# Layer 3's attention scores: the split queries stacked on 128 rows against the high keys, the low keys as a pair of 64-row products

## Chip, cores, metric

One NeuronCore of one Trainium2 chip. The metric is device time in microseconds (us) of one execution of the whole program; smaller is better.

## What is computed

Four layers in sequence on tokens `x` (2 x 1024 x 256) with a condition vector. Only layer 3's attention matters here; its part of the reference, cut:

```python
# on B = 2 sequences of N = 1024 tokens, D = 256;  H, HD = 16, 64
h = _ln(x, ln1_g, ln1_b) + shift
qkv = (h @ Wqkv.T).reshape(b, n, 3, H, HD)
q = _ln(qkv[:, :, 0].transpose(0, 2, 1, 3), qn_g, qn_b)
k = _ln(qkv[:, :, 1].transpose(0, 2, 1, 3), kn_g, kn_b)
v = qkv[:, :, 2].transpose(0, 2, 1, 3)
scores = jnp.einsum('bhnd,bhmd->bhnm', q, k) / jnp.sqrt(jnp.float32(HD))
attn = jax.nn.softmax(scores, axis=-1)
o = jnp.einsum('bhnm,bhmd->bhnd', attn, v)
x = x + o.transpose(0, 2, 1, 3).reshape(b, n, H * HD) @ Wout.T
...   # then a mixture of experts
```

## The kernel before

The program runs its stages one after another. Each stage has a block with one instruction stream per engine; the order within each is written out in the code, and semaphores tie the streams together. The two stages that the change touches are `layer3_qkv` (projections, normalisation of each head, writing of Q, K and V to device memory) and the heads stage of layer 3 (`heads_stage` with the class `Heads`), which follows it.

To keep the accuracy of 32 bits with the faster type float32r, an operand is split into a high part (rounded) and a low part (the rest), and a product is the sum of three: high x high, high x low, low x high. `PASSES = ((0, 0), (0, 1), (1, 0))` lists them. Device memory holds `l3_q` and `l3_k` as (part, head, 64, 1024): 64 features on rows, 1024 tokens along the row, each part 256 KB for a head.

`Heads` works through 32 heads (2 sequences x 16) of 8 turns each, 256 turns g in all; a turn has 128 queries t against 1024 keys. In SBUF a head has `Q` (128 partitions x 2 parts x 1024) and `K` (128 x 2 x 512). Partitions 0 to 63 and 64 to 127 both hold all the queries, in both parts; the keys are divided: the upper half has keys 0 to 511, the lower half keys 512 to 1023. So a product on rows 0 to 63 gives the scores of the first 512 keys, and one on rows 64 to 127 those of the others, and the two run in the array at once, as a pair. There are two such sets of tiles: `k3first` and `q3first` for even heads, `l3h_K` and `l3h_Q` for odd ones.

What each engine does in the heads stage:

- TensorE, for each g: `score(g)` (line 1477, six products of 512 columns; it waits for the exponentials of turn g - 2, and at a head's first turn for the head's loads), `turn(g - 3)` (line 1488, sixteen 64-row transposes of the probabilities into `ring`, waiting for the scaling and for both engines' copies of the turn before), and `mix` (line 1500, two products of the values with the transposed probabilities of the head before, each written as two instructions, with 128 rows and 64 columns of weights each). The mix starts at turn 11.
- VectorE: the negated maximum of each score row (line 1534), the inverse of the sum (line 1540), and the copy of one half of the transposes (line 1524).
- ScalarE: its half of the transposes (line 1526), the exponential with its sum (line 1558), and once a head `ocopy`, which copies the head's result to `osb` (line 1548). `osb` has two buffers; the copy of head n waits until the result of head n - 2 is stored.
- GpSimd: the scaling of the probabilities (line 1568), and in some turns a piece of the output weights' split.
- SP issues the transfers, in this order for each n: `load(n + 1)`, which is four times `load_head_part` (lines 1393 and 1394, one piece of Q and one of K), after the last score of head n - 1; `store(n - 2)` (line 1446, two transfers from `osb`); `load_v(n + 1)` (line 1440), after the mix of head n - 1; from n = 20 on for some heads one load of results for the next stage into `o3T` (line 1974).

In `layer3_qkv`, TensorE makes the sums of q, k and v for each tile of 128 tokens with products of 128 rows and 512 columns (line 2289), and transposes the normalised heads in 64-row halves (line 2256). Its inputs are a normalised chunk of 512 tokens in high and low parts, in two buffers (`NormTurnParts`). SP loads head 0's Q and K there, in four steps at the tiles 9 to 12 (`load_head_part` again).

Of the kernel before, what the change touches and what calls it, by code (L numbers as in the profile page):

```python
# [21 lines left out]
P = 128  # L22
# [1365 lines left out]
def load_head_part(sp, tiles, parts, n, part, hd, loaded):  # L1388

    (K, Q), (q, k) = tiles, parts  # L1390
    p_, c = divmod(part, 2)
    r = slice(c * hd, (c + 1) * hd)
    sp.dma_start(Q[r, p_, :].bitcast(F32), q[p_, n, :, :]).then_inc(loaded, 16)
    sp.dma_start(K[r, p_, :].bitcast(F32), k[p_, n, :, c * C:(c + 1) * C]).then_inc(loaded, 16)


class Heads:
# [3 lines left out]
    LOADS = 8  # L1401

    def __init__(self, s, parts, V, out, ident, hd, vscale, tiles, pending):
        self.V, self.out, self.ident, self.hd, self.vscale = V, out, ident, hd, vscale
        self.pending = pending
        self.K, self.Q = ([t, s.sb(n, shape, F32R)] for t, n, shape in zip(tiles, "KQ", ([P, 2, C], [P, 2, S])))
        self.vs = s.sb("vs", [P, 2, TB, hd])
        self.prob = s.sb("prob", [P, 4, S])
        self.pT = s.sb("pT", [P, 2, TB, S])
        self.osb = s.sb("osb", [P, 2, C])  # L1410
        self.nmax, self.total, self.inv = (s.sb(n, [P, 4]) for n in ("nmax", "total", "inv"))
        self.score = [s.ps(f"score{i}", (P, S)) for i in range(2)]
# [17 lines left out]
    def sp_program(self, sp):  # L1430
        def load(n):
            u = n % 2
            self.need(sp, self.scores, TB * (n - 1))
            for part in range(4):
                load_head_part(sp, (self.K[u], self.Q[u]), (self.q, self.k), n, part, self.hd, self.loaded[u])
# [7 lines left out]
        def store(n):  # L1443
            sp.wait_ge(self.ocopied, n + 1)
            for c in range(2):
                sp.dma_start(self.out[n, :, c * C:(c + 1) * C],
                             self.osb[c * self.hd:(c + 1) * self.hd, n % 2, :]).then_inc(self.stored[n % 2], 16)
# [19 lines left out]
    def pe_program(self, pe):  # L1467
        def score(g):
            n, t = divmod(g, TB)
            u = n % 2  # L1470
            if t == 0:
                self.need(pe, self.loaded[u], (n // 2 + u) * 16 * self.LOADS)
            self.need(pe, self.exps, g - 1)
            for i, (x, y) in enumerate(PASSES):
                for c in range(2):
                    r = slice(c * self.hd, (c + 1) * self.hd)
                    mm = pe.matmul(self.score[t % 2][:, c * C:(c + 1) * C], self.Q[u][r, x, t * P:(t + 1) * P],  # L1477
                                   self.K[u][r, y, :], start=i == 0, stop=i == 2)
            mm.then_inc(self.scores, 1)
# [64 lines left out]
    def act_program(self, act):  # L1544
        def ocopy(n):
            act.wait_ge(self.outs, n + 1)
            self.need(act, self.stored[n % 2], 32 * (n // 2))
            act.activation(self.osb[:, n % 2, :], self.ob[n % 2][:, :], ACT.Copy).then_inc(self.ocopied, 1)
# [620 lines left out]
class NormTurnParts(NormTurn):  # L2169

    def __init__(self, *args, **kw):
        super().__init__(*args, **kw)
        s, name = args[0], kw.get("name", "norm")
        self.parts = [s.sb(f"{name}_{n}", [P, self.bufs, KF, C], F32R) for n in ("hi", "lo")]
        self.written, self.split = s.sem(f"{name}_written"), s.sem(f"{name}_split")

    def act_scale(self, act, c):
# [3 lines left out]
        for kf in range(KF):  # L2181
            act.wait_ge(self.turned, c * KF + kf + 1)
            for to, sem in ((self.out[:, c % self.bufs, kf, :], self.written), (self.parts[0][:, c % self.bufs, kf, :], self.ready)):
# [3 lines left out]
    def dve_split(self, dve, c):  # L2187
        for kf in range(KF):
            dve.wait_ge(self.written, c * KF + kf + 1)
            dve.wait_ge(self.ready, c * KF + kf + 1)  # L2190
            dve.tensor_tensor(self.parts[1][:, c % self.bufs, kf, :], self.out[:, c % self.bufs, kf, :],
                              self.parts[0][:, c % self.bufs, kf, :].bitcast(F32), ALU.subtract).then_inc(self.split, 1)
# [5 lines left out]
def layer3_qkv(nc, sems, g, w, o):  # L2198
# [4 lines left out]
    with Stage(nc, sems, "l3qkv") as s:  # L2203
# [3 lines left out]
        nt = NormTurnParts(s, X, g["gain3"], g["shift3"], ident, [tb[:, kf * C:(kf + 1) * C] for kf in range(KF)], 1e-5)  # L2207
# [19 lines left out]
        def _(sp):  # L2227
            o.sp_results(sp, 1)
            o.sp_inverses(sp, 1)
            for tt in range(T):  # L2230
# [11 lines left out]
                if TB < tt <= TB + 4:  # L2242
                    load_head_part(sp, (g["k3first"], g["q3first"]), g["q3k3"], 0, tt - TB - 1, HD, early)
            sp.wait_ge(early, 8 * 16)

        @block.tensor
        def _(pe):
# [26 lines left out]
            for tt in range(T):  # L2274
# [3 lines left out]
                for j in range(6):  # L2278
# [8 lines left out]
                    for kf in range(KF):  # L2287
                        for p_, (x, y) in enumerate(PASSES):
                            mm = pe.matmul(sumb[i][:, half * C:(half + 1) * C], nt.parts[x][:, c % 2, kf, t * P:(t + 1) * P],
# [690 lines left out]
def build(nc, d, out):  # L2980
# [9 lines left out]
    with ExitStack() as always:  # L2990
# [22 lines left out]
        with ExitStack() as layer2:  # L3013
# [25 lines left out]
            with ExitStack() as weights3:  # L3039
                sb(weights3, "w3oT", [P, H * 64 // P * D])  # L3040
                sb(weights3, "k3first", [P, 2, C], F32R)
                sb(weights3, "q3first", [P, 2, S], F32R)
                with Semaphores(nc) as sems:
# [15 lines left out]
                    for name, shape, dt in (("o3T", [P, 2, H * 64 // P, C], F32), ("w3o_hi", [P, H * 64 // P * D], F32R),  # L3059
# [4 lines left out]
                                (g["k3first"], g["q3first"]), g["l3_pending"])  # L3064
# [24 lines left out]
```

## Time and profile before

| | |
|---|---|
| runs of the kernel | 2115.70, 2118.59, 2133.62 us (median 2118.59) |
| the profiled execution | 2115.73 us, span 2114.0 us |
| granted TensorE clock, mean over the span | 0.921 |
| busy share of the span | TensorE 89%, VectorE 70%, ScalarE 56%, GpSimd 38% |
| heads stage of layer 3 | first score at 1219.8, last at about 1830 us |

The profile is one execution, recorded by the hardware, with times from the span's start. PE is TensorE's products, PEld its weight loads, DVE is VectorE, ACT ScalarE, POOL GpSimd, SPq SP's transfers. A row names the line of the kernel, the output and inputs by the program's names, and the shape: `64*128 64x512` is a load of 64 rows by 128 columns of weights with 64 x 512 of the moving operand. "Idle before" tells how long the engine had nothing to do before a group, and what ended that. The end of a product is modelled: it holds the way through the array, so that products that follow closely overlap in the rows.

### The profile page before, as it was taken

To read this page: it belongs to the slowest core of one execution; us is meant where nothing else is said; L and a number is where in the kernel's file an instruction comes from. 1 tells how busy PE (TensorE), PEld (TensorE's weight loads), DVE (VectorE), ACT (ScalarE), POOL (GpSimd) and SP (SyncE) were. 2 spreads that over 40 slices of the span, in tenths; PEclk is the share of its full clock that TensorE was granted. 3 is DMA by queue.
4 is the path that set the end of the run, shared out by engine and by line. 5 is a ranking of instruction groups with operands and counts; after the bars stand their busy time and mean duration, and the time that the engine had idled before them with its cause. 6 is when DMAs were issued, how large, how long until landed. Compare 5 with 4: busy or idle time off the path is not lost. (4 is left out here: it accounts for less than half of the span.)

```text
span 2114.0 us, 37287 instructions
## 1 busy us (share of the span) xinstructions
PE 1873.8 (89%) x14338; PEld 1192.7 (56%) x14338; DVE 1483.4 (70%) x2500; ACT 1188.8 (56%) x2038; POOL 805.5 (38%) x724
## 2 busy tenths in 40 slices
PE   6988999788989999996888889999999999993786
PEld 3766577677533333333666655555555555492686
DVE  5665743564479897984688777777777777546796
ACT  3332332332228686884556677777777777632463
POOL 3465620174040302001245645554444444304376
PEclk8999999899959897998899989999999999996798
DMA  5000000100533211212256954454445555225453
GB/s 148 0 4 17 3 18 0 61 1 1 154 96 93 49 39 37 55 32 67 90 185 213 298 140 101 112 121 113 101 108 131 127 125 141 61 80 160 140 150 51
DMA packets 196833, 191.40 MB, mean 91 GB/s; under 512 B 64240, under 2 KB 155248, under 8 KB 196400
## 3 DMA queue, kind: packets, MB, share of 16 engines
q1 hardware_dynamic: 193584, 184.82, 32.4%
q0 software_dynamic: 3072, 4.20, 1.1%
q8 instruction: 114, 1.87, 0.4%
q14 instruction: 63, 0.52, 0.1%
HBM read 121.33 MB, written 67.37 MB: 89 GB/s over the span
## 5 line engine op out<-in xcount | busy, mean ns | idle before, releaser
L1568 POOL TENSOR_SCALAR l3h_prob<-l3h_prob,l3h_inv 128x1024 f32<-128x1024 f32 x256 | 288.2, 1126 | 320.8 <-DVE l3h_inv L1540 320.8
L1534 DVE TENSOR_REDUCE l3h_nmax<-l3h_score 128x1 f32<-128x1024 f32 x256 | 313.5, 1225 | 138.0 <-PE l3h_score L1477 137.9
L1758 DVE TENSOR_REDUCE l2h_nm<-l2h_rowb 128x1 f32<-128x1024 f32 x256 | 302.7, 1218 | 43.0 <-PE l2h_rowb L1689 42.7
L1793 ACT ACTIVATE l2h_pT<-l2h_score 128x512 f32<-128x512 f32 x512 | 274.7, 597 | 97.0 <-PE l2h_score L1711 74.5
L1558 ACT ACTIVATE l3h_prob<-l3h_score,l3h_nmax 128x1024 f32<-128x1024 f32 x256 | 285.8, 1117 | 38.5 <-DVE l3h_nmax L1534 3.6
L1500 PE MATMUL l3h_out<-l3h_pT,l3h_vs 128*64 128x512 f32 x1024 | 274.4, 617 | 0.0
L1526 ACT ACTIVATE l3h_pT<-l3h_ring 128x512 f32<-128x512 f32 x256 | 152.8, 597 | 104.4 <-PE l3h_ring L1488 103.9
L1488 PEld LDWEIGHTS l3h_ring<-ident,l3h_prob 64*128 64x128 f32 x4096 | 173.2, 139 | 35.5 <-issue 8.0
L1524 DVE COPY l3h_pT<-l3h_ring 128x512 f32<-128x512 f32 x256 | 172.1, 672 | 2.0 <-PE l3h_ring L1488 2.0
L1488 PE MATMUL l3h_ring<-ident,l3h_prob 64*128 64x64 f32 x4096 | 169.4, 222 | 2.2 <-DVE l3h_pT L1524 2.0
L1725 PE MATMUL l2h_out<-l2h_pT,l2h_vs 128*32 128x256 f32 (+1 forms) x1792 | 166.1, 445 | 0.0
L2492 POOL TENSOR_TENSOR l3qkv_lo<-l3qkv_full,l3qkv_hi 128x1024 fp32r<-128x1024 f32 x32 | 99.3, 3102 | 108.7 <-ACT l3qkv_hi L2327 108.7
L1477 PE MATMUL l3h_score<-k3first,q3first 64*128 64x512 f32 x768 | 125.0, 432 | 9.6 <-PEq L68 6.3
L1477 PEld LDWEIGHTS l3h_score<-k3first,q3first 64*128 64x128 f32 x768 | 63.7, 188 | 114.6 <-issue 99.8
L1477 PE MATMUL l3h_score<-l3h_K,l3h_Q 64*128 64x512 f32 x768 | 123.0, 425 | 2.5 <-DMA l3h_K<-l_k 2.3
L1477 PEld LDWEIGHTS l3h_score<-l3h_K,l3h_Q 64*128 64x128 f32 x768 | 62.1, 184 | 109.1 <-issue 96.0
L1689 PE MATMUL l2h_rowb<-l2K,l2Q 48*128 48x512 f32 x256 | 103.0, 499 | 13.8 <-PEq L68 9.6
L1711 PE MATMUL l2h_score<-l2Q,l2K 50*128 50x512 f32 x256 | 105.6, 497 | 0.5
L1807 POOL COPY l2h_vs<-V 128x128 f32<-128x128 f32 x32 | 8.3, 294 | 237.5 <-PE l2h_out L1725 237.5
L1689 PEld LDWEIGHTS l2h_rowb<-l2K,l2Q 48*128 48x128 f32 x256 | 44.6, 214 | 76.4 <-DVE l2h_nm L1758 60.6
L1725 PEld LDWEIGHTS l2h_out<-l2h_pT,l2h_vs 128*32 128x32 f32 x1792 | 36.4, 110 | 82.8 <-issue 51.2
L2380 DVE TENSOR_SCALAR l3qkv_full<-l3qkv_turns,headln 128x1024 f32<-128x1024 f32 x32 | 42.9, 1340 | 37.2 <-PE l3qkv_turns L2256 37.2
(456 smaller groups left out, 4354.4 us busy)
## 6 DMA issues: line engine op xcount, KB each, us to landing
q3first<-l_q SPq DMA_DIRECT2D x64, 256.0 KB, 5.1
l3h_Q<-l_q SPq DMA_DIRECT2D x64, 256.0 KB, 5.0
l_q<-l3qkv_hi SPq DMA_DIRECT2D x16, 512.0 KB, 4.7
l_q<-l3qkv_lo SPq DMA_DIRECT2D x16, 512.0 KB, 3.4
l_k<-l3qkv_hi SPq DMA_DIRECT2D x16, 512.0 KB, 3.0
l_k<-l3qkv_lo SPq DMA_DIRECT2D x16, 512.0 KB, 3.0
k3first<-l_k SPq DMA_DIRECT2D x64, 128.0 KB, 5.1
l3h_vs<-l_v SPq DMA_DIRECT2D x32, 256.0 KB, 3.1
```

Source lines behind the costliest of these rows:

```text
L1477: mm = pe.matmul(self.score[t % 2][:, c * C:(c + 1) * C], self.Q[u][r, x, t * P:(t + 1) * P], self.K[u][r, y, :], start=i == 0, stop=i == 2)
L1488: mm = pe.transpose(self.ring[half][:, kk * P // 2:(kk + 1) * P // 2], self.prob[r, g % 4, kk * P:(kk + 1) * P], self.ident[r, r])
L1500: mm = pe.matmul(self.ob[n % 2][c * self.hd:(c + 1) * self.hd, :], self.vs[:, n % 2, kk, :], self.pT[:, n % 2, kk, c * C:(c + 1) * C], sta ...
L1524: eng.tensor_copy(dst, src).then_inc(self.emptied_d, 1)
L1526: eng.activation(dst, src, ACT.Copy).then_inc(self.emptied_a, 1)
L1534: dve.tensor_reduce(self.nmax[:, t % 4:t % 4 + 1], self.score[t % 2][:, :], AX.X, ALU.max, negate=True).then_inc(self.maxes, 1)
L1558: act.activation(self.prob[:, q, :], self.score[g % 2][:, :], ACT.Exp, bias=self.nmax[:, q:q + 1], accum_out=self.total[:, q:q + 1]).then_ ...
L1568: pool.tensor_scalar(self.prob[:, q, :], self.prob[:, q, :], self.inv[:, q:q + 1], self.vscale, ALU.mult, ALU.mult).then_inc(self.scaled, 1)
L1689: mm = pe.matmul(self.rowb[h][:, c * C:(c + 1) * C], self.Q[u][r:r + self.SPLIT, t * P:(t + 1) * P], self.K[u][r:r + self.SPLIT, c * C:(c ...
L1725: mm = pe.matmul(self.ob[r:r + self.mw, at:at + w], self.vs[:, m % self.SLOTS, h, k, :], self.pT[:, g % 4, h, c * C + at:c * C + at + w], ...
L1758: dve.tensor_reduce(self.nm[:, mr % 2, at:at + 1], self.rowb[h][:, :], AX.X, ALU.max, negate=True).then_inc(self.maxes, 1)
L1793: act.activation(self.pT[:, g % 4, h, c * C:(c + 1) * C], self.score[v % 3][:, :], ACT.Exp).then_inc(self.exps, 1)
```

## The change

The queries and keys of a head are laid out differently, and the three parts of the score are made in another grouping.

- `Q[:, 0, :]` now has the high queries on partitions 0 to 63 and the low queries on 64 to 127. `K` has the high keys, all 1024, on both halves. One product over 128 rows gives high x high plus low x high at once, for 512 keys; two such products give the whole score row (`c` = 0, 1).
- The third part, high queries x low keys, stays a pair of 64-row products: `KL` has the low keys 0 to 511 on the upper half and 512 to 1023 on the lower, and the lower half needs the high queries too, which are loaded into `Q[64:128, 1]`.
- So a score has four products instead of six: full, full, and a pair. A head's loads are three of Q (256 KB each), two of K (256 KB) and two of `KL` (128 KB) where they were four of Q (256 KB) and four of K (128 KB).
- `K` and `KL` together need more room in SBUF. It is found by giving `osb` one buffer instead of two (the copy of head n now waits for the store of head n - 1), and by letting head 0's `KL` tile (`k3lo`) serve in `layer3_qkv` as one of the four pieces of the normalised chunk's low part.

The diff, without the changes of names in the calls:

```diff
 def load_head_part(sp, tiles, parts, n, part, hd, loaded):
-    (K, Q), (q, k) = tiles, parts
-    p_, c = divmod(part, 2)
-    r = slice(c * hd, (c + 1) * hd)
-    sp.dma_start(Q[r, p_, :].bitcast(F32), q[p_, n, :, :]).then_inc(loaded, 16)
-    sp.dma_start(K[r, p_, :].bitcast(F32), k[p_, n, :, c * C:(c + 1) * C]).then_inc(loaded, 16)
+    (K, KL, Q), (q, k) = tiles, parts
+    up, down = slice(0, hd), slice(hd, 2 * hd)
+    if part < 2:
+        r = (up, down)[part]
+        sp.dma_start(Q[r, 0, :].bitcast(F32), q[part, n, :, :]).then_inc(loaded, 16)
+        sp.dma_start(K[r, :, :].rearrange("p a c -> p (a c)").bitcast(F32), k[0, n, :, :]).then_inc(loaded, 16)
+    elif part == 2:
+        sp.dma_start(Q[down, 1, :].bitcast(F32), q[0, n, :, :]).then_inc(loaded, 16)
+    else:
+        for c, r in enumerate((up, down)):
+            sp.dma_start(KL[r, :].bitcast(F32), k[1, n, :, c * C:(c + 1) * C]).then_inc(loaded, 16)
...
 class Heads:
-    LOADS = 8
+    LOADS = 7
...
-        self.K, self.Q = ([t, s.sb(n, shape, F32R)] for t, n, shape in zip(tiles, "KQ", ([P, 2, C], [P, 2, S])))
+        self.Q = [tiles[2], s.sb("Q", [P, 2, S], F32R)]
...
-        self.osb = s.sb("osb", [P, 2, C])
+        self.K, self.KL = [tiles[0], s.sb("K", [P, 2, C], F32R)], [tiles[1], s.sb("KL", [P, C], F32R)]
+        self.osb = s.sb("osb", [P, C])
...
                 sp.dma_start(self.out[n, :, c * C:(c + 1) * C],
-                             self.osb[c * self.hd:(c + 1) * self.hd, n % 2, :]).then_inc(self.stored[n % 2], 16)
+                             self.osb[c * self.hd:(c + 1) * self.hd, :]).then_inc(self.stored[n % 2], 16)
...
-            for i, (x, y) in enumerate(PASSES):
-                for c in range(2):
-                    r = slice(c * self.hd, (c + 1) * self.hd)
-                    mm = pe.matmul(self.score[t % 2][:, c * C:(c + 1) * C], self.Q[u][r, x, t * P:(t + 1) * P],
-                                   self.K[u][r, y, :], start=i == 0, stop=i == 2)
+            for c in range(2):
+                pe.matmul(self.score[t % 2][:, c * C:(c + 1) * C], self.Q[u][:, 0, t * P:(t + 1) * P],
+                          self.K[u][:, c, :], start=True, stop=False)
+            for c in range(2):
+                r = slice(c * self.hd, (c + 1) * self.hd)
+                mm = pe.matmul(self.score[t % 2][:, c * C:(c + 1) * C], self.Q[u][r, c, t * P:(t + 1) * P],
+                               self.KL[u][r, :], start=False, stop=True)
             mm.then_inc(self.scores, 1)
...
             act.wait_ge(self.outs, n + 1)
-            self.need(act, self.stored[n % 2], 32 * (n // 2))
-            act.activation(self.osb[:, n % 2, :], self.ob[n % 2][:, :], ACT.Copy).then_inc(self.ocopied, 1)
+            self.need(act, self.stored[(n + 1) % 2], 32 * ((n + 1) // 2))
+            act.activation(self.osb[:, :], self.ob[n % 2][:, :], ACT.Copy).then_inc(self.ocopied, 1)
...
 class NormTurnParts(NormTurn):
-        self.parts = [s.sb(f"{name}_{n}", [P, self.bufs, KF, C], F32R) for n in ("hi", "lo")]
+        self.hi, lo = s.sb(f"{name}_hi", [P, self.bufs, KF, C], F32R), s.sb(f"{name}_lo", [P, self.bufs * KF - 1, C], F32R)
+        self.lo = [[first_low[:, :] if n == 0 else lo[:, n - 1, :] for n in range(u * KF, (u + 1) * KF)] for u in range(self.bufs)]
...
+    def part(self, x, c, kf):
+        return self.lo[c % self.bufs][kf] if x else self.hi[:, c % self.bufs, kf, :]
...
 def layer3_qkv(nc, sems, g, w, o):
                 if TB < tt <= TB + 4:
-                    load_head_part(sp, (g["k3first"], g["q3first"]), g["q3k3"], 0, tt - TB - 1, HD, early)
-            sp.wait_ge(early, 8 * 16)
+                    load_head_part(sp, (g["k3first"], g["k3lo"], g["q3first"]), g["q3k3"], 0, tt - TB - 1, HD, early)
+            sp.wait_ge(early, 7 * 16)
```

## Rows read from the trace of the kernel before

**Rows 1.** The page: its header and part 1.

```profile
span 2114.0 us, 37287 instructions
...
PE 1873.8 (89%) x14338; PEld 1192.7 (56%) x14338; DVE 1483.4 (70%) x2500; ACT 1188.8 (56%) x2038; POOL 805.5 (38%) x724
```

**Rows 2.** Busy time of each engine in two stretches, granted clock, DMA.

```profile
1400.00:1600.00 200.00, 200.00 (x2180) 113.86 (x2180) 157.18 (x250) 155.02 (x262) 94.10 (x84) 1.00 0.49 112
640.00:700.00 60.00, 59.33 (x524) 21.78 (x520) 57.30 (x57) 52.30 (x99) 1.60 (x6) 1.00 0.38 95
```

**Rows 3.** Timeline of one turn: start us, duration us, engine, line, operation [idle before].

```profile
1502.39 0.96 PE L1477 MATMUL l3h_score<-l3h_K,l3h_Q 64*128 64x512 f32 x6
1502.96 0.74 PEld L1488 LDWEIGHTS l3h_ring<-ident,l3h_prob 64*128 64x128 f32 x16
...
1503.39 1.23 DVE L1534 TENSOR_REDUCE l3h_nmax<-l3h_score 128x1 f32<-128x1024 f32 x1 [0.51 <-PE l3h_score L1477]
...
1504.61 0.67 DVE L1524 COPY l3h_pT<-l3h_ring 128x512 f32<-128x512 f32 x1
...
1504.78 0.53 PEld L1477 LDWEIGHTS l3h_score<-l3h_K,l3h_Q 64*128 64x128 f32 x6 [0.81 <-issue]
...
1505.36 0.74 PEld L1488 LDWEIGHTS l3h_ring<-ident,l3h_prob 64*128 64x128 f32 x16
```

**Rows 4.** Timeline in four short windows of that turn.

```profile
1502.39 0.50 PE L1477 MATMUL l3h_score<-l3h_K,l3h_Q 64*128 64x512 f32 x2
...
1502.73 0.62 PE L1477 MATMUL l3h_score<-l3h_K,l3h_Q 64*128 64x512 f32 x4
...
1503.78 0.65 PE L1500 MATMUL l3h_out<-l3h_pT,l3h_vs 128*64 128x512 f32 x2
...
1504.26 0.60 PE L1500 MATMUL l3h_out<-l3h_pT,l3h_vs 128*64 128x512 f32 x2
```

**Rows 5.** Line L1477 from 1243 to 1850: durations ns min/median/max; who waited (us, times).

```profile
L1477 PE MATMUL l3h_score<-l3h_K,l3h_Q x744: 386/390/501, 1243.9 to 1830.8; 64*128 64x512 f32 x186
...
  DVE l3h_nmax L1534: 129.5, 244
```

**Rows 6.** Timeline in layer 3's projections, TensorE's products, then its weight loads.

```profile
1200.57 0.39 PE L2289 MATMUL l3qkv_k_sum<-w3lo,l3qkv_norm_hi 128*128 128x512 f32 x1
1200.80 0.40 PE L2289 MATMUL l3qkv_k_sum<-w3hi,l3qkv_norm_lo 128*128 128x512 f32 x1
...
1201.77 0.50 PE L2289 MATMUL l3qkv_v_sum<-w3hi,l3qkv_norm_hi 128*128 128x512 f32 x1
1202.11 0.39 PE L2289 MATMUL l3qkv_v_sum<-w3lo,l3qkv_norm_hi 128*128 128x512 f32 x1
...
1201.13 0.58 PEld L2256 LDWEIGHTS l3qkv_turns<-ident,l3qkv_xn 64*128 64x128 f32 x16 [0.36 <-issue]
1201.77 0.19 PEld L2289 LDWEIGHTS l3qkv_v_sum<-w3hi,l3qkv_norm_hi 128*128 128x128 f32 x1
```

**Rows 7.** Timeline of TensorE in the stage's first turns.

```profile
1238.62 0.71 PE L1488 MATMUL l3h_ring<-ident,l3h_prob 64*128 64x64 f32 x16 [0.33 <-DVE l3h_pT L1524]
```

**Rows 8.** Waits from 1260 to 1840: us in all, times, longest us.

```profile
PEld l3h_score L1477 <- DMA l3h_K<-l_k: 7.5, 6, 2.0
PEld l3h_score L1477 <- DMA k3first<-l_k: 5.9, 5, 1.7
```

**Rows 9.** Timeline around the start of a late head.

```profile
1644.19 0.36 SPq L1440 DMA_DIRECT2D l3h_vs<-l_v  x1
...
1649.63 0.60 SPq L1394 DMA_DIRECT2D l3h_K<-l_k  x1
...
1650.27 1.23 SPq L1446 DMA_DIRECT2D l_heads_out<-l3h_osb  x2
...
1657.26 0.96 PE L1477 MATMUL l3h_score<-l3h_K,l3h_Q 64*128 64x512 f32 x6 [1.12 <-DMA l3h_K<-l_k]
...
1665.41 0.59 ACT L1548 ACTIVATE l3h_osb<-l3h_out 128x512 f32<-128x512 f32 x1
```

More of the change, by code:

```diff
@@ L1434, in load @@
             for part in range(4):
-                load_head_part(sp, (self.K[u], self.Q[u]), (self.q, self.k), n, part, self.hd, self.loaded[u])
+                load_head_part(sp, (self.K[u], self.KL[u], self.Q[u]), (self.q, self.k), n, part, self.hd, self.loaded[u])
         def load_v(n):
@@ L2169, with __init__ @@
 class NormTurnParts(NormTurn):
-    def __init__(self, *args, **kw):
+    def __init__(self, first_low, *args, **kw):
         super().__init__(*args, **kw)
         s, name = args[0], kw.get("name", "norm")
-        self.parts = [s.sb(f"{name}_{n}", [P, self.bufs, KF, C], F32R) for n in ("hi", "lo")]
+        self.hi, lo = s.sb(f"{name}_hi", [P, self.bufs, KF, C], F32R), s.sb(f"{name}_lo", [P, self.bufs * KF - 1, C], F32R)
+        self.lo = [[first_low[:, :] if n == 0 else lo[:, n - 1, :] for n in range(u * KF, (u + 1) * KF)] for u in range(self.bufs)]
         self.written, self.split = s.sem(f"{name}_written"), s.sem(f"{name}_split")
@@ L2182, in act_scale @@
             act.wait_ge(self.turned, c * KF + kf + 1)
-            for to, sem in ((self.out[:, c % self.bufs, kf, :], self.written), (self.parts[0][:, c % self.bufs, kf, :], self.ready)):
+            for to, sem in ((self.out[:, c % self.bufs, kf, :], self.written), (self.hi[:, c % self.bufs, kf, :], self.ready)):
                 act.activation(to, self.banks[kf][:, :], ACT.Identity, bias=self.shift[:, kf, b:b + 1],
@@ L2190, in dve_split @@
             dve.wait_ge(self.ready, c * KF + kf + 1)
-            dve.tensor_tensor(self.parts[1][:, c % self.bufs, kf, :], self.out[:, c % self.bufs, kf, :],
-                              self.parts[0][:, c % self.bufs, kf, :].bitcast(F32), ALU.subtract).then_inc(self.split, 1)
+            dve.tensor_tensor(self.lo[c % self.bufs][kf], self.out[:, c % self.bufs, kf, :],
+                              self.hi[:, c % self.bufs, kf, :].bitcast(F32), ALU.subtract).then_inc(self.split, 1)
+    def part(self, x, c, kf):
+        return self.lo[c % self.bufs][kf] if x else self.hi[:, c % self.bufs, kf, :]
     def wait_split(self, eng, c):
@@ L2206, in layer3_qkv @@
         sumb = [s.ps(f"{n}_sum", (P, W)) for n in ("q", "k", "v")]
-        nt = NormTurnParts(s, X, g["gain3"], g["shift3"], ident, [tb[:, kf * C:(kf + 1) * C] for kf in range(KF)], 1e-5)
+        nt = NormTurnParts(g["k3lo"], s, X, g["gain3"], g["shift3"], ident, [tb[:, kf * C:(kf + 1) * C] for kf in range(KF)], 1e-5)
         qk = s.sb("qk", [P, 2, 2 * W])
@@ L2288, in _ @@
                         for p_, (x, y) in enumerate(PASSES):
-                            mm = pe.matmul(sumb[i][:, half * C:(half + 1) * C], nt.parts[x][:, c % 2, kf, t * P:(t + 1) * P],
+                            mm = pe.matmul(sumb[i][:, half * C:(half + 1) * C], nt.part(x, c, kf)[:, t * P:(t + 1) * P],
                                            wp[y][:, (kf * 6 + j) * C:(kf * 6 + j + 1) * C],
@@ L3042, in build @@
                 sb(weights3, "q3first", [P, 2, S], F32R)
+                sb(weights3, "k3lo", [P, C], F32R)
                 with Semaphores(nc) as sems:
@@ L3063, in build @@
                     heads_stage(nc, sems, g, "l3h", Heads, g["q3k3"], g["v3"], o3, 64, 1.0, lambda s: o,
-                                (g["k3first"], g["q3first"]), g["l3_pending"])
+                                (g["k3first"], g["k3lo"], g["q3first"]), g["l3_pending"])
                     project_out(nc, sems, g, "l3o", o)
```

## The prediction

> **What bounds the kernel now.** I read the page's header and engine shares first [rows 1]: the profiled execution took 2115.73 us for a span of 2114.0 us, so 1.7 us lie outside the span, and TensorE is busy 89% of it. The change sits in the heads stage of layer 3, so the next view is the busy time by stretch [rows 2]: in the 200 us from 1400 to 1600 TensorE has work in flight for all 200.00 us, while no other engine reaches 80%, and its granted clock is 1.00. A busy TensorE is not proof of a full one, so the third view is one turn (128 queries of one head) in order of time [rows 3]. Its score starts at 1502.39 and the next one at 1504.78, a turn of 2.39 us; between them TensorE loads the first transpose weights at 1502.96, and the mix starts at 1503.78 [rows 4].
>
> The short windows take the score apart [rows 4]. Its six products are three pairs (rows 0 to 63 and 64 to 127 at once). The first pair lasts 0.50 us, the other four products 0.62 together; by the line's own durations [rows 5] a product takes 390 ns when its weights were loaded behind another one and up to 501 when not. So 0.11 us of the first load is in the open, and the pairs follow each other at 0.23 us (0.62 less 0.39): 0.11 + 3 x 0.23 = 0.80 us for the score.
>
> One gap is of interest. The mix's first pair lasts 0.65 us and its second 0.60, so 0.05 of a load is in the open, and a pair streams for 1504.26 - 1503.78 - 0.05 = 0.43 us. The second is through at 1504.69; the score's weights load at 1504.78, 0.09 us later, with another 0.11 in the open. That is 0.20 us each time the array goes from the mix's shape (128 rows by 64 columns) to the score's (64 by 128). From score to transposes, both 64 by 128, there is none: the transpose weights load at 1502.96, 0.57 into the score, which is when its third pair starts (0.11 + 2 x 0.23). So a change of shape costs 0.2 us here, a change of operands nothing.
>
> VectorE is nearly as tight. Its reduce of a score starts at 1503.39, behind the score's end, and its copy out of the transposes ends at 1504.61 + 0.67 = 1505.28; the next turn's transposes wait for that copy and load their weights at 1505.36, 0.08 us later [rows 3]. The reduce waits for TensorE 244 times, 129.5 us in all [rows 5]: 0.53 us a turn.
>
> **The change part by part.**
> 1. Two of the three 64-row pairs go, and two full 128-row products come, each with a load: four products and four loads become two and two. In columns nothing changes: a pair is one passage of 512 columns, and so is one full product. Its price stands in the layer 3 projections [rows 6]: starts at 1200.57 and 1200.80, 0.23 us apart, each with its own 128 x 128 load. So 2 x 0.23 replaces 2 x 0.23: 0. A rule makes it dearer: the Trainium skill, "TensorE: Matmul & The Clock Gate", Part 3, The mechanism, says that a weight load overlaps products in flight only when the row group differs. By it the second full product would show its load, and the sum would be 0.11 us a turn higher. The rows speak against it: 0.23 from start to start, load included.
> 2. Added is a change of shape inside the score, from the full products to the last pair of 64 rows. The projections have it, from full products to the 64-row head transposes [rows 6]: last full product at 1200.80, next load at 1201.13, 0.33 us where 0.23 is usual, a gap of 0.10. The load of the following pair then lies in the open, 0.11 for such weights. Together 0.21, beside the 0.20 of mix to score in this very loop. Ends: 0 (score to transposes, same shape), and 0.23, if the full product is reckoned at its bare columns (half of 0.43, the mix streaming twice as long a column) and not at 0.23. I take 0.20. What the Trainium skill says of it ("TensorEngine Tiling (Array Packing)", Key Properties): a change of tiling mode drains the engine; its list has 128 x 128, 128 x 64 and 64 x 128 as modes of their own, so by it the change adds one drain a turn and removes none, and where the trace shows such a change it agrees.
> 3. Mix to the first score product: before 128 x 64 to 64 x 128, after 128 x 64 to 128 x 128. No row shows that one. Nearest are mix to score (0.20) and, with a full product as the target, transposes to projection [rows 6]: load at 1201.77, first product 0.50 us, again 0.11 in the open. Ends: 0.20 less (the load hides behind the mix, both using all rows), and nothing. I take nothing, as both nearest rows pay.
> 4. Who is late next: nobody. VectorE needs 1505.28 - 1503.39 = 1.89 us from the reduce to the copy's end; at 2.59 us a turn it has 0.2 more room.
> 5. Where it doesn't count: the stage's first turns have no mix, and there the transposes wait for VectorE's copy (0.33 us at 1238.62 [rows 7]), against two changes of shape, 0.4: under 1 us in all, taken as 0. So 244 turns count, the number of waits in [rows 5].
> 6. Loads: Q and K are 1536 KB a head before and after, in 7 loads instead of 8, all on SP's queue, which has one issue of 0.60 us less; the wait for them keeps its place. In late heads, where a load of results stands ahead of them in the queue, the next head's first score waits: the last K load is issued at 1649.63, and the score starts at 1657.26, 1.1 us late [rows 9]. The waits put down to these loads are 7.5 + 5.9 us, in 11 entries [rows 8]; each holds 0.81 that the weight queue is idle in any turn [rows 3], so the loss is 13.4 - 8.9 = 4.5 us. From the release of the queue (V's load at 1644.19) to the head's due start lie 5 turns, 1.0 us more after the change, and one issue less is 0.6 more: this covers nearly all. -4.4, ends 0 and -4.5.
> 7. One result buffer for two: ScalarE's copy of a head's result now waits until the previous one is stored. Behind it on ScalarE stand its half of the transposes and the next exponentials, and TensorE waits for both. The store is issued from 1650.27, two issues of 0.6, and the next copy comes at 1665.41 [rows 9]: 13.9 us for two transfers of 128 KB, the size for which the last K load needed up to 7.6 (1649.63 to 1657.26). Cost 0; should the cover be gone, the missing part of it once a head.
> 8. The projection stage's low parts at another place, and the early loads of head 0 in another order, with one issue less: 0, since they carry the same bytes to the same point.
>
> **Sum.** 244 x 0.20 = 48.8 us, less 4.4: +44.4. Against the profiled 2115.73 that is 2160.1. The shown runs are 2115.70, 2118.59 and 2133.62, so the profiled one is at their low end and a median may stand a little higher: 2161 us.
>
> **The rivals.**
> - A, mix to full product is no change of shape to the array: the first load hides behind the mix, -0.20, and pays for the one inside the score. The turn stays 2.39, and the issue that is saved takes a microsecond or so off the late heads: 2115 us. For it: both use all 128 rows, and no row shows this pair. Against: the others pay. It decides if less than 0.09 us a turn is left. This is the end on the other side, not slower. 7%.
> - B, full to pair is free: also 2115 us. Against it the gap at 1201.13 [rows 6]; for it, that load also waits for VectorE, which could be the gap. 5%.
> - C, both: TensorE needs 2.19, and VectorE's loop takes over. Its copy leaves 0.08 us, and the transposes' load could come some 0.1 later and still be behind the third pair (0.23): a turn of 2.21 to 2.31, -20 to -44 us, about 2084. 2%.
> - D, a full product's load lies in the open after all: 0.31 a turn, 75.6 - 4.5 = +71: 2187 us. Against it the 0.23 of [rows 6]. 4%.
> - E, TensorE's clock falls to 1.2 GHz at times, since the array now pauses more: each such stretch costs up to its length again, so over 2165. In layer 2's heads, where a turn also changes shape between scores and mix, it is 1.00 over 60 us [rows 2]: 1%.
>
> **How the numbers follow.** The forecast has 81%; its own range is 0.16 to 0.23 us a turn, with or without the late heads' waits: 2150 to 2173. A and B lie 45 us below with 12%, D and E above with 5%, C with 2%. 8 in 10 is the forecast with room for a gap partly covered and for runs like the one at 2133: 2143 to 2182. A measurement of this kernel can tell about 1%, 21 us, from no change. Faster by more: C, 2%. Within: A, B and a little of the forecast's low side, 13%. Slower: 85%.
>
> **What would show it.** From score to score 2.59 us; the two full products 0.23 apart; the pair's weight load 0.33 after the second full product, its first products 0.50 long; the reduce idle for 0.7 a turn; waits for K at late heads gone or under 0.3; no wait for a store; the clock 1.00; 512 products fewer. It is wrong if the turn stays at 2.39 (a first product of 0.39 behind the mix would be A, one of 0.39 inside the score B), if the second full product starts over 0.3 behind the first (D), or if a wait for K or a store stands at a head's start.

## The result: 2.2% slower, and the profile after

The changed kernel takes 2161.27 us (median of 4 runs, 2155.39 to 2169.39) against 2117.14 us for the kernel before (4 runs, 2114.80 to 2133.62). The comparison by fast runs alone gives a ratio of 1.0222, with a 95% interval of 1.0187 to 1.0256 (the two medians by themselves stand 1.0208 apart). So the kernel is slower beyond doubt; whether by more or less than 2% the interval leaves open. The forecast was 2161, the range 2143 to 2182. The profiled execution of the changed kernel took 2164.81 us.

The page's header and engine shares, as in [rows 1], and the line of the transfers that the program issues itself:

```profile
span 2163.1 us, 36232 instructions
...
PE 1922.9 (89%) x13826; PEld 1172.2 (54%) x13826; DVE 1484.5 (69%) x2500; ACT 1190.3 (55%) x2038; POOL 803.6 (37%) x724
...
q1 hardware_dynamic: 191024, 184.82, 31.6%
```

TensorE has 13826 products and as many loads where it had 14338: 512 fewer, two of each in 256 turns. It is busy for 49 us more with fewer instructions, and its share is 89% as before. So fewer instructions didn't mean less time here. The transfers carry the same 184.82 MB as on the page of before, in 191024 packets for 193584.

Where the time went is read from the busy time by stretch, with the stretches cut at the same events in both kernels: first score, first score after the first mix, last score, first product of the next stage, end. Columns as in [rows 2]. Before:

```profile
1219.80:1243.90 24.10, 20.55 (x220) 13.68 (x220) 20.46 (x32) 19.35 (x33) 11.62 (x11) 0.82 0.80 182
1243.90:1830.20 586.30, 582.31 (x6320) 330.69 (x6319) 457.30 (x730) 451.23 (x760) 280.46 (x251) 1.00 0.48 114
1830.20:1850.60 20.40, 14.36 (x120) 5.98 (x119) 5.45 (x10) 7.36 (x13) 3.73 (x5) 0.97 0.12 27
1850.60:2114.00 263.40, 190.75 (x1402) 175.77 (x1402) 180.58 (x545) 115.84 (x250) 121.86 (x125) 0.81 0.41 117
```

After:

```profile
1216.80:1242.60 25.80, 24.06 (x197) 13.28 (x197) 20.56 (x32) 19.53 (x33) 11.70 (x11) 0.81 0.74 164
1242.60:1873.60 631.00, 630.21 (x5833) 310.80 (x5833) 457.13 (x729) 452.01 (x760) 278.45 (x252) 1.00 0.45 105
1873.60:1894.20 20.60, 14.57 (x119) 5.88 (x117) 5.46 (x10) 7.37 (x13) 3.65 (x5) 0.95 0.12 27
1894.20:2163.10 268.90, 192.21 (x1402) 177.09 (x1402) 181.16 (x545) 116.02 (x250) 122.36 (x125) 0.81 0.40 114
```

The turns with a mix take 631.0 us where they took 586.3: +44.7, and +44.4 was forecast. The rest of the span's difference (2163.1 - 2114.0 = 49.1) is small pieces: 3.0 less ahead of the stage, 1.7 more in its first turns, 0.2 behind the last score, and 5.5 in the experts, whose code is the same in both. The clock in the turns is 1.00 in both kernels.

One turn in order of time, which answers to [rows 3]:

```profile
1499.92 0.50 PE L1486 MATMUL l3h_score<-l3h_KL,l3h_Q 64*128 64x512 f32 x2
...
1501.85 0.73 PE L1482 MATMUL l3h_score<-k3first,q3first 128*128 128x512 f32 x2
1502.51 0.19 PEld L1486 LDWEIGHTS l3h_score<-k3lo,q3first 64*128 64x128 f32 x2 [0.36 <-issue]
1502.51 0.50 PE L1486 MATMUL l3h_score<-k3lo,q3first 64*128 64x512 f32 x2
1502.64 0.66 PEld L1497 LDWEIGHTS l3h_ring<-ident,l3h_prob 64*128 64x128 f32 x14
...
1503.05 1.23 DVE L1543 TENSOR_REDUCE l3h_nmax<-l3h_score 128x1 f32<-128x1024 f32 x1 [0.71 <-PE l3h_score L1486]
```

The pair's products start at 1499.92 and at 1502.51: a turn of 2.59 us. The two full products, begun at 1501.85, take 0.73 together. The second one, in a short window:

```profile
1502.18 0.40 PE L1482 MATMUL l3h_score<-k3first,q3first 128*128 128x512 f32 x1
```

It starts 0.33 after the first: 0.11 of the first product's own load, as for the pairs in [rows 4] (1502.39 and 1502.73), and 0.23 of its columns. Its own load is hidden (0.40, not 0.50). Then comes the pair's weight load at 1502.51, 0.33 after the second product where 0.23 is usual: a gap of 0.10. The load queue itself stood idle for 0.36 us before it, without a wait for another engine ("issue" at line 1486, below). The pair's products last 0.50, so their load lies in the open. The transposes' load (1502.64) follows inside the pair with no gap. VectorE's reduce starts at 1503.05 after 0.71 us of idleness, 0.51 in [rows 3].

The transition for which the trace of before had no row, from the mix to a full product, in a short window:

```profile
1503.91 0.60 PE L1509 MATMUL l3h_out<-l3h_pT,l3h_vs 128*64 128x512 f32 x2
...
1504.44 0.30 PEld L1482 LDWEIGHTS l3h_score<-k3first,q3first 128*128 128x128 f32 x2 [0.81 <-issue]
1504.44 0.50 PE L1482 MATMUL l3h_score<-k3first,q3first 128*128 128x512 f32 x1
```

The second mix pair starts at 1503.91 and the load 0.53 later, at 1504.44, as before the change (1504.26 to 1504.78 in [rows 3, 4]); and the first full product lasts 0.50, its load in the open. Line 1486 over the whole stretch, to be set beside [rows 5] (durations in ns; who waited, in us and times):

```profile
L1486 PE MATMUL l3h_score<-l3h_KL,l3h_Q x248: 493/497/497, 1243.2 to 1874.2; 64*128 64x512 f32 x124
...
  issue: 88.9, 244
...
  DVE l3h_nmax L1543: 174.6, 244
```

A first product of 493 to 497 ns in every turn: this load is never hidden. The idle time before it is 0.36 us in each of the 244 turns (88.9 us), and the reduce's wait has grown from 129.5 to 174.6 us. Both totals are 244 turns' worth, one entry a turn.

### The profile page after: what moved, and what is told of

It is laid out like the page before. It is cut to its first block and busy times, and to the rows that moved or that the text cites. A ratio compares the mean times of both kernels' runs of the same rounds, so it can differ in the third digit from the quotient of the medians.

```text
span 2163.1 us, 36232 instructions
## 1 busy us (share of the span) xinstructions
PE 1922.9 (89%) x13826; PEld 1172.2 (54%) x13826; DVE 1484.5 (69%) x2500; ACT 1190.3 (55%) x2038; POOL 803.6 (37%) x724
## 3 DMA queue, kind: packets, MB, share of 16 engines
q1 hardware_dynamic: 191024, 184.82, 31.6%
## 5 line engine op out<-in xcount | busy, mean ns | idle before, releaser
L1497 PEld LDWEIGHTS l3h_ring<-ident,l3h_prob 64*128 64x128 f32 x4096 | 166.9, 139 | 23.4 <-issue 6.2
L1482 PE MATMUL l3h_score<-k3first,q3first 128*128 128x512 f32 x256 | 96.0, 457 | 8.7 <-PEq L68 8.0
L1482 PEld LDWEIGHTS l3h_score<-k3first,q3first 128*128 128x128 f32 x256 | 39.1, 192 | 108.0 <-issue 104.3
L1482 PE MATMUL l3h_score<-l3h_K,l3h_Q 128*128 128x512 f32 x256 | 93.7, 447 | 0.8 <-DMA l3h_KL<-l_k 0.8
L1482 PEld LDWEIGHTS l3h_score<-l3h_K,l3h_Q 128*128 128x128 f32 x256 | 38.1, 188 | 101.8 <-issue 98.2
```

The costliest lines, as they stand in the source:

```text
L1497: mm = pe.transpose(self.ring[half][:, kk * P // 2:(kk + 1) * P // 2], self.prob[r, g % 4, kk * P:(kk + 1) * P], self.ident[r, r])
```

## The experiments

The distances from score to score (the turn) are medians over the turns with a mix, where nothing else is said. Experiments 2, 3, 5, 6 and 7 were run once each; what they show is read from their turns, and their times stand beside.

**1. The new tiles with the old shape.** Everything of the change stays (layout, seven loads, one result buffer), and only the two full products go back to 64-row pairs. The low queries of the lower half stand in for operands that this layout hasn't in place.

```diff
-            for c in range(2):
-                pe.matmul(self.score[t % 2][:, c * C:(c + 1) * C], self.Q[u][:, 0, t * P:(t + 1) * P],
-                          self.K[u][:, c, :], start=True, stop=False)
+            for x in range(2):
+                for c in range(2):
+                    r = slice(c * self.hd, (c + 1) * self.hd)
+                    pe.matmul(self.score[t % 2][:, c * C:(c + 1) * C], self.Q[u][r, 0, t * P:(t + 1) * P],
+                              self.K[u][r, c, :], start=x == 0, stop=False)
```

> The changed kernel with its tiles, its seven loads and its single result buffer, but the two full 128-row products are written as two pairs of 64-row products on the same tiles (the low queries of the lower half stand in for operands that this layout has not in place, so the scores are not the reference's). If the change of shape inside the score is the whole cost, a turn is back at 2.39 us and the time at 2110 to 2120 us, with the waits for loads at late heads still about 4 us in all. If the layout, the loads or the single buffer cost it, the turn stays at 2.59 and the time near 2161.

Measured: 2112.21 us against 2111.96 for the kernel before, run beside it, ratio 0.9995 (0.9966 to 1.0024). Timeline of TensorE:

```profile
1500.00 0.72 PE L1484 MATMUL l3h_score<-l3h_K,l3h_Q 64*128 64x512 f32 x4
1500.56 0.39 PE L1488 MATMUL l3h_score<-l3h_KL,l3h_Q 64*128 64x512 f32 x2
...
1502.39 0.73 PE L1484 MATMUL l3h_score<-l3h_K,l3h_Q 64*128 64x512 f32 x4
```

The last pair starts 0.56 after the score and lasts 0.39: its load is hidden again. The turn is 2.39. The whole loss of the change is gone with the change of shape, and layout, loads and the single buffer cost nothing that can be measured.

**2. The pair first.** The same four products in another order, which adds one change of shape a turn.

```diff
-            for c in range(2):
-                pe.matmul(self.score[t % 2][:, c * C:(c + 1) * C], self.Q[u][:, 0, t * P:(t + 1) * P],
-                          self.K[u][:, c, :], start=True, stop=False)
             for c in range(2):
                 r = slice(c * self.hd, (c + 1) * self.hd)
-                mm = pe.matmul(self.score[t % 2][:, c * C:(c + 1) * C], self.Q[u][r, c, t * P:(t + 1) * P],
-                               self.KL[u][r, :], start=False, stop=True)
+                pe.matmul(self.score[t % 2][:, c * C:(c + 1) * C], self.Q[u][r, c, t * P:(t + 1) * P],
+                          self.KL[u][r, :], start=True, stop=False)
+            for c in range(2):
+                mm = pe.matmul(self.score[t % 2][:, c * C:(c + 1) * C], self.Q[u][:, 0, t * P:(t + 1) * P],
+                               self.K[u][:, c, :], start=False, stop=True)
```

> The changed kernel with the 64-row pair ahead of the two full products: the same four products, but one more change of shape a turn (mix to pair, pair to full, full to transposes, transposes to mix). If each change costs a gap of 0.10 us and the load in the open (0.05 for the transposes' weights), the turn is 2.59 + 0.15 = 2.74 us, the time about 2161 + 37 = 2198. If full products as such were the cost, the turn stays at 2.59 and the time at 2161.

Measured: 2199.05 us in one run, turn 2.75. Timeline of TensorE:

```profile
1499.52 0.50 PE L1483 MATMUL l3h_score<-l3h_KL,l3h_Q 64*128 64x512 f32 x2
1499.95 0.73 PE L1486 MATMUL l3h_score<-l3h_K,l3h_Q 128*128 128x512 f32 x2
1500.61 0.71 PE L1497 MATMUL l3h_ring<-ident,l3h_prob 64*128 64x64 f32 x16
...
1502.27 0.50 PE L1483 MATMUL l3h_score<-l3h_KL,l3h_Q 64*128 64x512 f32 x2
```

From pair (1499.52) to full (1499.95) there are 0.43 us: 0.11 of the pair's load, its 0.23, and 0.09 of gap. The first full product behind the pair has its load in the open as well (0.73 for two). From there to the transposes there are 0.66 us. Every boundary between 64-row and 128-row products is paid for, in both directions.

**3. The kernel before without its third pair.** Low queries x high keys is left out. This looks for the floor under TensorE's time.

```diff
-            for i, (x, y) in enumerate(PASSES):
+            for i, (x, y) in enumerate(PASSES[:2]):
...
-                                   self.K[u][r, y, :], start=i == 0, stop=i == 2)
+                                   self.K[u][r, y, :], start=i == 0, stop=i == 1)
```

> The kernel before without its third pair (low queries x high keys is left out of the score). TensorE alone would need 2.39 - 0.23 = 2.16 us a turn, 56 us less. If VectorE's loop comes next, as estimated for rival C, the turn ends at 2.21 to 2.31 us instead, 20 to 44 us less than before: about 2085.

Measured: 2074.58 us in one run. Turns are alternately about 2.17 and 2.24, mean 2.21, not 2.16. Timeline:

```profile
1500.35 0.67 DVE L1524 COPY l3h_pT<-l3h_ring 128x512 f32<-128x512 f32 x1
...
1500.54 0.73 PE L1477 MATMUL l3h_score<-k3first,q3first 64*128 64x512 f32 x4
1501.10 0.60 PEld L1488 LDWEIGHTS l3h_ring<-ident,l3h_prob 64*128 64x128 f32 x16 [0.26 <-issue]
...
1502.78 0.30 PEld L1477 LDWEIGHTS l3h_score<-k3first,q3first 64*128 64x128 f32 x4 [0.81 <-issue]
```

The transposes' weight load at 1501.10 comes 0.08 us after VectorE's copy has ended (1500.35 + 0.67 = 1501.02): VectorE's loop decides now. That is the lower end of the range estimated for rival C. The turns with a mix took 549.0 us in all where they had taken 586.3, and the time fell by 37 us. At 0.18 us a turn it would be 44; the shorter heads wait longer for their loads (below).

**4. The mixes in twos.** If changes of shape cost, doing them half as often should gain. In the kernel before, two turns' mixes are done every second turn, between score and transposes:

```diff
             gt = g - self.LAG
-            if 0 <= gt < TB * self.N:
-                turn(gt)
             n, kk = divmod(gt - TB, TB)
-            if n >= 0:
+            if n >= 0 and kk % 2:
+                mix(n, kk - 1)
                 mix(n, kk)
+            if 0 <= gt < TB * self.N:
+                turn(gt)
```

> The kernel before with the mixes of two turns done together every second turn, between score and transposes: two changes of shape in two turns instead of four. If a pair of changes costs 0.34 us (0.14 before the mix, 0.20 behind it), TensorE needs 0.17 us less a turn on average, 2.22; with VectorE's loop close behind, 2.25, and the time about 2117 - 35 = 2082. The rival: the turns are now uneven, VectorE and ScalarE wait in one and are late in the other, and the mean turn stays at 2.39 or above: 2117 or more.

Measured: 2176.36 us, ratio 1.0279 (1.0230 to 1.0329): slower. Turns alternate between 3.28 and 2.00 to 2.10 us, about 2.65 on average. The rival was right. Timeline:

```profile
1501.34 0.71 PE L1488 MATMUL l3h_ring<-ident,l3h_prob 64*128 64x64 f32 x16
...
1502.09 0.69 DVE L1525 COPY l3h_pT<-l3h_ring 128x512 f32<-128x512 f32 x1 [1.21 <-PE l3h_ring L1488]
1502.12 0.60 ACT L1527 ACTIVATE l3h_pT<-l3h_ring 128x512 f32<-128x512 f32 x1 [2.11 <-PE l3h_ring L1488]
1502.61 1.11 ACT L1559 ACTIVATE l3h_prob<-l3h_score,l3h_nmax 128x1024 f32<-128x1024 f32 x1
...
1502.85 0.60 PEld L1488 LDWEIGHTS l3h_ring<-ident,l3h_prob 64*128 64x128 f32 x16 [0.48 <-issue]
...
1503.86 0.53 PEld L1477 LDWEIGHTS l3h_score<-l3h_K,l3h_Q 64*128 64x128 f32 x6 [0.41 <-ACT l3h_prob L1559]
```

VectorE and ScalarE can't empty the transposes before TensorE has made them, which now comes after a double mix: they stood idle 1.21 and 2.11 us. ScalarE's exponential stands behind that copy in its queue (1502.61), and the next score but one waits for it (0.41 us at 1503.86). The transposes' load at 1502.85 comes 0.07 after VectorE's copy has ended (1502.09 + 0.69), some 0.4 later than the score ahead of it (from 1501.86) would have let it. These two waits are nearly all of the difference between the 5.31 us that two turns took and the 2 x 2.22 that TensorE was reckoned to need. What the array saved in changes, its neighbours lost by waiting. The edit does two things, though: it doubles the mixes and moves them ahead of the transposes. Doubled mixes in the old place weren't run.

**5. Full, pair, full.** Five changes of shape a turn in place of three; the pair stands between the two full products (where the diff has "..."), opening the sum of the second half of the keys and closing that of the first.

```diff
-            for c in range(2):
-                pe.matmul(self.score[t % 2][:, c * C:(c + 1) * C], self.Q[u][:, 0, t * P:(t + 1) * P],
-                          self.K[u][:, c, :], start=True, stop=False)
+            pe.matmul(self.score[t % 2][:, 0 * C:1 * C], self.Q[u][:, 0, t * P:(t + 1) * P],
+                      self.K[u][:, 0, :], start=True, stop=False)
...
+            mm = pe.matmul(self.score[t % 2][:, 1 * C:2 * C], self.Q[u][:, 0, t * P:(t + 1) * P],
+                           self.K[u][:, 1, :], start=False, stop=True)
```

> The changed kernel with its four products in the order full (keys 0 to 511), pair, full (the other keys): five changes of shape a turn where the changed kernel has three. If each has its own price, the turn is 2.59 + 0.20 (pair to full) + 0.15 (full to transposes) = 2.94 us, and the time about 2161 + 244 x 0.35 = 2246. If a drain were paid once a turn however often the shape changes, or if two of them overlapped, it is 2.75 as in the pair-first order, 2199.

Measured: 2258.54 us in one run, turn 2.95. Timeline of TensorE:

```profile
1503.47 0.50 PE L1481 MATMUL l3h_score<-k3first,q3first 128*128 128x512 f32 x1
1503.90 0.51 PE L1485 MATMUL l3h_score<-k3lo,q3first 64*128 64x512 f32 x2
1504.34 0.49 PE L1487 MATMUL l3h_score<-k3first,q3first 128*128 128x512 f32 x1
1504.77 0.71 PE L1498 MATMUL l3h_ring<-ident,l3h_prob 64*128 64x64 f32 x16
```

Each step inside the score is 0.43 to 0.44 us (1503.47, 1503.90, 1504.34, 1504.77), where a passage of 512 columns takes 0.23. So the prices add up and none overlaps another. The time is 12 us above the 2246 expected, and that lies in the stage's first turns, which take 3.22 us each instead of 1.9. The stretch from the first score to the first one after a mix, columns as in [rows 2]:

```profile
1217.80:1255.40 37.60, 36.89 (x197) 18.95 (x197) 20.76 (x32) 20.14 (x34) 12.31 (x11) 0.50 0.53 117
```

It is 11.8 us longer than the changed kernel's 25.80, and the granted clock in it is 0.50 (1.2 GHz) all through, where the changed kernel had 0.81 on average. What these turns would have cost at the full clock isn't shown, nor why the clock rose later.

**6. Full products only.** The low keys' pair is left out, to be set beside experiment 3, which passes the same columns as two pairs.

```diff
             for c in range(2):
-                pe.matmul(self.score[t % 2][:, c * C:(c + 1) * C], self.Q[u][:, 0, t * P:(t + 1) * P],
-                          self.K[u][:, c, :], start=True, stop=False)
-            for c in range(2):
-                r = slice(c * self.hd, (c + 1) * self.hd)
-                mm = pe.matmul(self.score[t % 2][:, c * C:(c + 1) * C], self.Q[u][r, c, t * P:(t + 1) * P],
-                               self.KL[u][r, :], start=False, stop=True)
+                mm = pe.matmul(self.score[t % 2][:, c * C:(c + 1) * C], self.Q[u][:, 0, t * P:(t + 1) * P],
+                               self.K[u][:, c, :], start=True, stop=True)
```

> The changed kernel without the low keys' pair (high queries x low keys is left out of the score): two full products a turn, to be set against the kernel before with two of its pairs, 2.21 us a turn. TensorE would need 2.59 - 0.23 - 0.20 + 0.15 = 2.31 us, with the change of shape now between the full products and the transposes. If full products save something over pairs that the third pair hides, the turn is at VectorE's 2.21 or less.

Measured: 2086.05 us in one run, turn 2.31 (2.21 in experiment 3). Timeline of TensorE:

```profile
1501.88 0.73 PE L1482 MATMUL l3h_score<-k3first,q3first 128*128 128x512 f32 x2
1502.54 0.71 PE L1493 MATMUL l3h_ring<-ident,l3h_prob 64*128 64x64 f32 x16
...
1504.19 0.50 PE L1482 MATMUL l3h_score<-k3first,q3first 128*128 128x512 f32 x1
```

Two full products take 0.66 us with the way to the transposes; two pairs in experiment 3 had 0.56 to the transposes' load (1500.54 to 1501.10), which waited for VectorE. Full products save nothing over pairs.

**7. Four full products.** In place of the changed kernel's four products, the pair is written as two more full products on the same tiles (high keys stand in for low ones): no 64-row product is left in the score.

```diff
+            for x in range(2):
+                for c in range(2):
+                    mm = pe.matmul(self.score[t % 2][:, c * C:(c + 1) * C], self.Q[u][:, 0, t * P:(t + 1) * P],
+                                   self.K[u][:, c, :], start=x == 0, stop=x == 1)
```

> The changed kernel with the pair written as two more full products on the same tiles (high keys stand in for the low ones, which would need to lie on both halves, so the scores are not the reference's). It pays one passage of 512 columns more than the changed kernel, 0.23 us, and trades the change inside the score, 0.20, for one before the transposes, 0.15: a turn of 2.77 us, 244 x 0.18 = 44 more, about 2205. If the second of two full products had its load in the open, it would show as 0.34 us between them, and the turn as 3.0 or more.

Measured: 2210.93 us in one run, turn 2.78. Timeline of TensorE:

```profile
1501.01 1.19 PE L1483 MATMUL l3h_score<-k3first,q3first 128*128 128x512 f32 x4
1502.13 0.72 PE L1494 MATMUL l3h_ring<-ident,l3h_prob 64*128 64x64 f32 x16
...
1503.79 0.73 PE L1483 MATMUL l3h_score<-l3h_K,l3h_Q 128*128 128x512 f32 x2
```

Four take 1.19 us to the end of the last, that is 0.50 + 3 x 0.23. A weight load between full products is hidden, so rival D falls for good. Full rows throughout cost 0.19 us a turn more than the changed kernel: one passage of columns more, and still three changes of shape.

**8. The results' load behind the head's own loads.** In the kernel before, the transfer into `o3T` moves from the end of SP's step to behind the next step's `load`.

```diff
             if n + 1 < self.N:
                 load(n + 1)
+            if 0 <= n - 1 - self.PREFETCH < NC // B * self.side.LOADS:
...
+                self.side.sp_load(sp, *divmod(n - 1 - self.PREFETCH, self.side.LOADS))
             if n >= 2:
                 store(n - 2)
             if n + 1 < self.N:
                 load_v(n + 1)
-            if 0 <= n - self.PREFETCH < NC // B * self.side.LOADS:
...
-                self.side.sp_load(sp, *divmod(n - self.PREFETCH, self.side.LOADS))
```

> The kernel before with the late heads' load of results issued behind the next head's Q and K loads instead of ahead of them. If that load causes the late waits (4.5 us in all), they go, the turn stays 2.39, and the time falls by 4 us, 0.2%, at the edge of what can be measured: the trace has to show it. If the waits come from the amount of data alone, they stay or move to other heads.

Measured: 2109.73 us against 2114.80, ratio 0.9984 (0.9955 to 1.0013): no difference that can be measured in the whole. The waits of the weight queue for these loads, as in [rows 8]:

```profile
PEld l3h_score L1477 <- DMA l3h_K<-l_k: 2.7, 3, 0.9
...
PEld l3h_score L1477 <- DMA k3first<-l_k: 1.6, 2, 0.8
```

They are 4.3 us in 5 entries of which each holds the usual 0.81, so 0.2 us of loss remain of 4.5, and the turns with a mix, from the first to the last score, take 582.1 us instead of 586.3. The cause is right and, by one trace of each, worth 4 us.

## Why the prediction was right, and where its sizes were off

Orders and distances from score to score in one table (a time stands beside the kernel before as run with it: 2117 for the changed one, 2112 for experiments 1 and 2, 2115 for 5 and 7):

| kernel | order in a turn | turn, us | time, us |
|---|---|---|---|
| before | pair x 3, transposes, mix | 2.39 | 2117 |
| experiment 1 | pair x 3, transposes, mix | 2.39 | 2112 |
| after | full x 2, pair, transposes, mix | 2.59 | 2161 |
| experiment 2 | pair, full x 2, transposes, mix | 2.75 | 2199 |
| experiment 7 | full x 4, transposes, mix | 2.78 | 2211 |
| experiment 5 | full, pair, full, transposes, mix | 2.95 | 2259 |

- Part 1, full products in place of pairs at no gain: right. A product behind another full one adds 0.23 us, its load hidden. The sign that was set for rival D, a second full product over 0.3 behind the first, was set wrongly: it forgot the first product's own load of 0.11, and by its words the 0.33 measured would speak for D. With D's load in the open it would have been 0.45. The rule that a load overlaps only products of another row group (the Trainium skill, "TensorE: Matmul & The Clock Gate", Part 3, The mechanism) would have given 0.11 us more a turn, and experiment 7 with four of them in a row shows none of it.
- Part 2, the change of shape inside the score at 0.20 us: right, 2.59 less 2.39. Experiment 1 takes it away and the loss goes; experiments 2 and 5 add one or two more and pay 0.15 and 0.35, as worked out from the same two parts, gap and open load. That the engine drains when the tiling mode changes (the Trainium skill, "TensorEngine Tiling (Array Packing)", Key Properties) agrees with every one of these. Rival B falls: no semaphore stands at this load, and the gap is there. A rival that wasn't named, that a product waits because it adds to sums which the one before it has just written, falls too: the pairs of experiment 1 do that and show no gap, while full products to transposes (experiment 6) and mix to score have the gap and write elsewhere.
- Part 3, mix to full product costs what mix to pair did: right, 0.53 us between the second mix pair and the load, and 0.50 for the first product. This was the one transition that no row showed, and rival A hung on it.
- Part 4, nobody is late next: right. VectorE's reduce had 0.2 us a turn more of idleness ahead of it.
- Part 5, the first turns are free: nearly. That stretch is 1.7 us longer. The granted clock stayed at 0.50 for about 9.9 us of it, where it had been 8.5; how much of the 1.7 is that and how much the changes of shape wasn't separated.
- Part 6, the late heads' waits: the mechanism is right, the size a little over. 4.4 us were to go. The waits after the change:

```profile
ACT l3h_osb L1557 <- PE l3h_out L1509: 6.7, 2, 6.3
...
PEld l3h_score L1482 <- DMA l3h_KL<-l_k: 3.3, 3, 1.7
...
PEld l3h_score L1482 <- DMA k3lo<-l_k: 1.6, 2, 0.8
```

Their excess over 0.81 an entry is 4.9 - 4.1 = 0.8 us, so 3.7 went. What is left stands at a single head, whose score waits 1.7 - 0.8 = 0.9 us for the low keys, where the prediction allowed no wait over 0.3. Experiment 1, with the new loads and the old turn, has 10.8 us in 9 entries, 3.5 in excess: so of the 3.7, about 1.0 would be due to the loads' new form and the rest to the longer heads, by one trace of each. Experiments 3 and 6 close the loop from the other side: with shorter heads the waits rose to about 12 and 11 us.
- Part 7, the single buffer: right. ScalarE's copy waits only for the mix at the stage's end (6.7 us in 2 entries above, as before), never for a store; the store's issue and the next copy of a late head:

```profile
1681.11 1.23 SPq L1453 DMA_DIRECT2D l_heads_out<-l3h_osb  x2
...
1697.32 0.59 ACT L1557 ACTIVATE l3h_osb<-l3h_out 128x512 f32<-128x512 f32 x1
```

From 1681.11 to 1697.32 are 16.2 us, for transfers that land 5.6 us after their issue (median of the stage).
- Part 8, nothing in the projection stage: nothing that can be told apart. The first score starts at 1202.6 to 1222.3 us in the six profiles with the changed stage and at 1215.6 to 1231.9 in the four with the old one.
- Rival C's floor, 2.21 to 2.31 us, was measured at 2.21 (experiment 3). Rival E: the clock stayed at 1.00 in the turns with a mix. Nor does the rest of the program's clock explain the loss: its mean was 0.921 over 2114.0 us and 0.923 over 2163.1, which is 334 and 333 us at the lower level.
- What no step had: 5.5 us in the experts, and 3.0 less before the heads stage, within the spread of part 8. The experts' code is the same in both kernels, and the runs of one kernel differ by more (2155 to 2169). That spread goes, by and large, with the clock: the four runs of the changed kernel had mean granted clocks of 0.920, 0.923, 0.926 and 0.927 at spans of 2167.7, 2163.1, 2153.7 and 2156.0 us. For the 5.5 us no cause was sought.

That the median came out within 0.3 us of 2161 is luck, with runs 14 us apart: between the two profiled executions the difference is 49.1 us and not 44.4. The net of the turns, +44.7 for +44.4, is so close because two small misses nearly cancel: 3.7 us came back from the waits and not 4.4, and the turns cost 0.199 us each, 48.4 in 243 distances, and not 48.8.

The best of the versions measured is the kernel before with its results' load moved (experiment 8), 4 us by the trace and not shown by the run times. Changing shape less often than twice a turn was tried once (experiment 4), and moved the loss to the neighbours.

## What to carry to other kernels

Count a stream's passages of columns and its changes of shape, not its instructions: here two 64-row products side by side took the same 0.23 us as one of 128 rows, so merging them gained nothing, while each boundary between 64-row and 128-row products, or between full and split columns, cost 0.15 to 0.2 us with the weight load behind it. Before regrouping products, look what stands on either side of them in the queue and keep equal shapes together, provided that the engines which feed on them don't have to wait for it. And when a head or tile gets shorter, look again at the loads that just made it: here 0.1 to 0.2 us off a turn brought 6 to 8 us of new waits (experiments 6 and 3).

## What the runs showed of the hardware beyond the forecast

- The gap at a change of shape was the same in each direction and for both types of operand (float32r in the scores, float32 in transposes and mix): 0.09 to 0.10 us from full to pair, pair to full, full to transposes and mix to full. What differs is the load in the open, 0.11 us for 128 columns of float32r weights (products of 0.50 where 0.39 is usual), 0.05 for the mix's (0.65 and 0.60 in [rows 4]) and for the transposes', the latter from the turns of experiments 2 and 7, which leave 0.15 to 0.16 for gap and load together.
- Two changes 0.43 us apart are paid in full, both of them (experiment 5).
